# Sorting only the edge numbers and gathering the ends of the edges per tile, in a four-stage graph network

## The reference

```python
row, col = src, dst
edge_feature = silu(edge_rbf @ We1 + be1) @ We2 + be2     # 20625 x 128 -> 512
msg = edge_feature * x[col]                               # x is relu(layernorm(x)) here
agg = segment_sum(msg, row, num_segments=625)
return x + (silu(agg @ Wn1 + bn1) @ Wn2 + bn2)
```

## Time and profile before

| | |
|---|---|
| median of 3 runs | 1199.06 us |
| the profiled execution, its span | 1200.69 us, 1198.9 us |
| busy, share of the span | PE 97%, DVE 71%, ACT 57%, POOL 35% |
| chain that ended last | PE 88%, DVE 6%, ACT 3%, issue 1%, DMA 1% |
| granted TensorE clock, mean | 0.989 of full speed |
| HBM | 86.52 MB read, 8.85 MB written |

### The profile page before, as it was taken

One profiled execution on the slowest core, in us unless ns is written; L12 is line 12 of the kernel. 1 busy time (PEld: TensorE's weight loads), 2 busy tenths in 40 slices (PEclk: granted clock), 3 DMA queues, 4 the chain that ended last, 5 costly groups with the idle time before them and its releaser, 6 DMA issues.

```text
span 1198.9 us, 20918 instructions
## 1 busy us (share of the span) xinstructions
PE 1158.1 (97%) x6268; PEld 970.2 (81%) x6268; DVE 851.5 (71%) x1479; ACT 680.5 (57%) x1351; POOL 418.6 (35%) x546
## 2 busy tenths in 40 slices
PE   6989899999999999999999999998899999999997
PEld 3658788888888888888888888886789888798786
DVE  8767777777777777777777777777977234175664
ACT  3567567676676766767676676765734223142352
POOL 2001555565546555555555555551500000001000
PEclk9999999999999999999999999999899999999999
DMA  5544622222222222222222322221101202022101
GB/s 192 205 154 158 234 87 72 83 82 71 87 74 79 80 74 85 70 85 77 76 85 68 87 74 79 82 72 36 44 1 37 71 8 97 0 71 71 44 2 44
DMA packets 26966, 95.88 MB, mean 80 GB/s; under 512 B 6533, under 2 KB 6783, under 8 KB 22578
## 3 DMA queue, kind: packets, MB, share of 16 engines
q0 software_dynamic: 18592, 54.42, 15.2%
q1 hardware_dynamic: 8208, 40.84, 9.5%
q10 hardware_dynamic: 130, 0.13, 0.0%
HBM read 86.52 MB, written 8.85 MB: 80 GB/s over the span
## 4 chain that ended last, share of the span: by engine, by line
PE 88%; DVE 6%; ACT 3%; issue 1%; DMA 1%; DVEq 0%; SPq 0%; ACTq 0%
PE ps L1004 13%; PE ps L1006 12%; PE ps L1005 12%; PE ps L997 9%; PE ps L999 9%; PE ps L998 9%; PE ps L1012 3%; PE ps L1011 3%; PE ps L1111 3%; PE ps L1110 3%; PE ps L1050 3%; PE ps L1115 2%; PE ps L1038 1%; PE ps L1247 1%; PE ps L1065 1%
## 5 line engine op out<-in xcount | busy, mean ns | idle before, releaser
L1004 PE MATMUL ps<-we_hi,s_hi 128*128 128x512 f32 x664 | 268.7, 405 | 0.0
L1006 PE MATMUL ps<-we_hi,s_lo 128*128 128x512 f32 x664 | 260.2, 392 | 0.0
L1005 PE MATMUL ps<-we_lo,s_hi 128*128 128x512 f32 x664 | 260.1, 392 | 0.0
L578 POOL DMA_INDIRECT xg<-h_dram,node_picks x166 | 177.0, 1066 | 96.7 <-POOL node_picks L568 66.1
L720 ACT ACTIVATE m_hi<-msg 128x512 fp32r<-128x512 f32 x166 | 105.0, 632 | 156.9 <-DVE msg L1667 92.9
L572 POOL DMA_INDIRECT rbf<-in_edge,edge_picks x166 | 171.5, 1033 | 50.5 <-issue 33.5
L1672 DVE TENSOR_TENSOR m_lo<-msg,m_hi 128x512 fp32r<-128x512 f32 x166 | 114.9, 692 | 59.3 <-ACT m_hi L720 58.6
L1660 DVE TENSOR_TENSOR s_lo<-s,s_hi 128x1024 fp32r<-128x1024 f32 x83 | 101.8, 1226 | 75.5 <-ACT s_hi L714 50.3
L1006 PEld LDWEIGHTS ps<-we_hi,s_lo 128*128 128x128 f32 x664 | 124.9, 188 | 28.6
L1005 PEld LDWEIGHTS ps<-we_lo,s_hi 128*128 128x128 f32 x664 | 125.7, 189 | 21.1
L1004 PEld LDWEIGHTS ps<-we_hi,s_hi 128*128 128x128 f32 x664 | 125.3, 189 | 21.4
(11 more groups left out here) (301 smaller groups left out, 2556.4 us busy)
## 6 DMA issues: line engine op xcount, KB each, us to landing
stage<-in_fold_a SPq DMA_DIRECT2D x6, 1024.0 KB, 5.1
stage<-in_fold_b SPq DMA_DIRECT2D x6, 1024.0 KB, 8.6
fold_dram<-folded SPq DMA_DIRECT2D x6, 1024.0 KB
wstage<-fold_dram SPq DMA_DIRECT2D x6, 1024.0 KB, 4.9
w_raw<-in_nodew SPq DMA_DIRECT2D x3, 1024.0 KB, 7.2
wstage<-in_selfw SPq DMA_DIRECT2D x3, 1024.0 KB, 5.0
rbf<-in_edge,edge_picks POOLq DMA_INDIRECT x166
xg<-h_dram,node_picks POOLq DMA_INDIRECT x166
```

What stands on the lines that cost most here:

```text
L578: pool.indirect_dma_start(xg[t.slot][:, j], None, h_dram, bass.IndirectOffsetOnAxis(ap=node_picks[t.slot][:, j:j + 1], axis=0)).then_inc(x ...
L1004: pe.matmul(outp, lh, rh, start=False, stop=False, skip_group_check=True)
L1005: pe.matmul(outp, lh, rl, start=False, stop=False, skip_group_check=True)
L1006: return pe.matmul(outp, ll, rh, start=False, stop=False, skip_group_check=True)
```

## The change

- **Sorting.** Only the edge numbers are still moved by matmuls. `ended` and its multiplications on VectorE and matmuls on TensorE are gone. GpSimd writes both ends of all edges side by side (`ends_i`), and SyncE saves them as a table of 8 bytes per edge in DRAM (`ends_dram`), with a row ahead of the first for slots without an edge.
- **Gathers.** `slot_picks` has the edge number and the number plus one side by side. `gather_edges` issues two gathers of rows of the table (`ends`) ahead of the two of `rbf`; `pick_nodes` takes the destinations from `ends`.
- **Columns.** `srccol`, `dstcol`, `dstval` are made per step, two steps ahead (`column_firsts`, `column_seconds`), four VectorE operations on 128x2. The counts are packed as lower and upper half of the nodes instead of even and odd, so the flush reads its 16-bit halves with a stride.
- **Folds.** The three unsplit folds have buffers of their own (`plain`), and the factors of folds 0 to 4 are loaded at once. The last quarter of the factors of each split fold is split ahead of the marks and one-hots of that unit, not behind them.
- **Clearing.** `acc_agg` and half of `acc_adj` are cleared by GpSimd at the start, the rest later by VectorE.

```diff
@@ sync
             load_factors(0)
             load_factors(1)
             sp.dma_start(x_res[:], a["x"].rearrange("(c p) f -> p c f", p=NC)).then_inc(x_in, 16)
-            sp.wait_ge(fold_mm, K)
-            load_factors(2)
+            for m in range(2, FOLDS - 1):
+                load_factors(m)
+            sp.wait_ge(ends_joined, 4)
+            sp.dma_start(ends_dram[1:E + 1].rearrange("(p t) v -> p t v", p=EP), ends_i[:]).then_inc(ends_saved, 16)
+            sp.dma_start(ends_dram[0:1], no_ends[:]).then_inc(ends_saved, 16)
             save_product(0)
@@ gpsimd
+            pool.memset(acc_agg[:], 0.0).then_inc(acc_zeroed, 1)
+            pool.memset(acc_adj[:, 0:late_zero], 0.0).then_inc(acc_zeroed, 1)
...
             def pick_edges(t):
                 t.wait(pool, rT_mm, 1, -1)
-                pool.tensor_copy(edge_picks[t.slot][:], slot_edge[:, bass.ds(t.count(2), 2)]).then_inc(picked, 1)
+                t.wait(pool, cols_made, 4, -4)
+                pool.tensor_copy(edge_picks[t.slot][:].rearrange("p j v -> p (j v)"),
+                                 slot_picks[:].rearrange("p t v -> p (t v)")[:, bass.ds(t.count(4), 4)]).then_inc(picked, 1)
             def pick_nodes(t):
                 t.wait(pool, msg_ready, 2, -2)
-                pool.tensor_copy(node_picks[t.slot][:], slot_dst[:, bass.ds(t.count(2), 2)]).then_inc(picked, 1)
+                pool.wait_ge(ends_in[t.slot], t.rounds(32))
+                pool.sem_inc(ends_landed, 1)
+                pool.tensor_copy(node_picks[t.slot][:], ends[t.slot][:, :, 1]).then_inc(picked, 1)
             def gather_edges(t):
                 for j in range(2):
                     pool.indirect_dma_start(
+                        ends[t.slot][:, j], None, ends_dram,
+                        bass.IndirectOffsetOnAxis(ap=edge_picks[t.slot][:, j, 1:2], axis=0)).then_inc(ends_in[t.slot], 16)
+                for j in range(2):
+                    pool.indirect_dma_start(
                         rbf[t.slot][:, j], None, a["edge"],
@@ vector, hots(i)
-                for v in range(2):
-                    mm = dve.tensor_tensor(ended[r][:, v], hot_lo[r][:],
-                                           pairs[:, v, :, None].to_broadcast([EP, GROUP // 2, P, 2]), op=ALU.mult)
-                mm.then_inc(ends_made, 1)
@@ vector and scalar, the woven units
+                if u == K - 1 and WHOLE <= m + 1 < FOLDS:
+                    factor_low(m + 1, u)
                 if n + 1 < len(units):
                     for i in AFTER[units[n + 1][0]][units[n + 1][1]]:
                         hots(i)
...
-                if WHOLE <= m + 1 < FOLDS:
+                if u < K - 1 and WHOLE <= m + 1 < FOLDS:
                     factor_low(m + 1, u)
@@ vector, the edge step
+            def column_firsts(t):
+                s = t.slot
+                dve.wait_ge(ends_in[s], t.rounds(32))
+                t.wait(dve, hots_ready, 3, -3)
+                dve.tensor_tensor(srccol[s][:], ends[s][:, :, 0], tile_base[:, bass.ds(t.count(2), 2)],
+                                  op=ALU.subtract).then_inc(cols_made, 1)
+                dve.tensor_scalar(upper[s][:], ends[s][:, :, 1], float(ND), None, ALU.is_ge).then_inc(cols_made, 1)
...
                     rows_lo(t.at(2))
+                    column_firsts(t.at(2))
                 message(t, 0)
+                if ahead:
+                    column_seconds(t.at(2))
```

More of the change, by code:

```diff
@@ L264, in build @@
         iota_d = main("iota_d", [P, ND + 1], F16)
-        dstval = main("dstval", [P, TILES], F32)
-        odd_i = main("odd_i", [P, TILES], I32)
-        half_i = main("half_i", [P, TILES], I32)
         loop = Region(main.at)
-        edge_picks = [loop(f"edge_picks{i}", [P, 2], I32) for i in range(2)]
+        edge_picks = [loop(f"edge_picks{i}", [P, 2, 2], I32) for i in range(2)]
+        ends = [loop(f"ends{i}", [P, 2, 2], I32) for i in range(2)]
+        srccol = [loop(f"srccol{i}", [P, 2], F32) for i in range(2)]
+        upper = [loop(f"upper{i}", [P, 2], F32) for i in range(2)]
+        dstcol = [loop(f"dstcol{i}", [P, 2], F32) for i in range(2)]
+        dstval = [loop(f"dstval{i}", [P, 2], F32) for i in range(2)]
         node_picks = [loop(f"node_picks{i}", [P, 2], I32) for i in range(2)]
@@ L414, in build @@
         weights_hi, weights_lo = sem("weights_hi"), sem("weights_lo")
-        stage_in = [sem(f"stage_in{i}") for i in range(2)]
+        stage_in = [sem(f"stage_in{m}") for m in range(FOLDS)]
         split_hi, split_lo = sem("split_hi"), sem("split_lo")
@@ L468, in load_factors @@
             def load_factors(m):
+                factors = plain[m] if m < WHOLE else stage[m % 2]
                 for part, w in enumerate((a["fold_a"], a["fold_b"])):
-                    sp.dma_start(stage[m % 2][:, part].rearrange("p k f -> p (k f)"), w[m]).then_inc(stage_in[m % 2], 16)
+                    sp.dma_start(factors[:, part].rearrange("p k f -> p (k f)"), w[m]).then_inc(stage_in[m], 16)
             def save_product(m):
@@ L485, in _ @@
             sp.dma_start(row_a[:], a["be2"].to_broadcast([P, F])).then_inc(small_in, 16)
[L486 to L496, removed]
+            save_product(1)
+            sp.wait_ge(split_lo, K)
+            load_factors(FOLDS - 1)
+            sp.wait_ge(ln_act, 1 + C)
+            sp.dma_start(h_dram.rearrange("(c p) f -> p c f", p=NC), h32[:]).then_inc(h_saved, 16)
+            for m in range(2, FOLDS):
                 save_product(m)
@@ L1565, in hots @@
                                       op=ALU.is_equal).then_inc(made, 1)
-                pairs = ends16[:, :, i * GROUP:i * GROUP + GROUP].rearrange("p v (j u) -> p v j u", u=2)
-                dve.wait_ge(hots_lo_made, i + 1)
-                for v in range(2):
-                    mm = dve.tensor_tensor(ended[r][:, v], hot_lo[r][:],
-                                           pairs[:, v, :, None].to_broadcast([EP, GROUP // 2, P, 2]), op=ALU.mult)
-                mm.then_inc(ends_made, 1)
             def factor_low(m, k):
@@ L1703, in flush_agg, with dst_order, adj_rows @@
                 return b
+            def dst_order(pairs):
+                return pairs[:].bitcast(U16)[:, 0:NP].rearrange("p (n two) -> p two n", two=2)
+            def adj_rows(b):
+                return acc_adj[:, bass.ds(b * NP, NP)].rearrange("p (two n) -> p two n", two=2)
             def flush_adj(t, b):
@@ L1757, in edge_step @@
                     silu_lo(t.at(1))
-                if t.reg is not None or t.c + 2 < STEPS:
+                ahead = t.reg is not None or t.c + 2 < STEPS
+                if ahead:
                     rows_lo(t.at(2))
+                    column_firsts(t.at(2))
                 message(t, 0)
+                if ahead:
+                    column_seconds(t.at(2))
                 if full:
```

120 lines of the change are left out of this document (60 added, 60 removed).

## The result

The changed kernel takes 1254.24 us, the median of four runs (1247.66 to 1260.94), against 1199.27 of the kernel before on the same chip: 1.0463 times as long, 95% interval 1.0423 to 1.0503. Forecast were 1262, with a range of 1208 to 1298. The profiled execution is the one of 1249.35 us (span 1247.6).

A forecast was written before the change was run, and what follows sets the result against it. TensorE paced the loop before; GpSimd would after, at 9.33 us a step. Start, 80 steps, landing and tail gave +52.4, stalls +11: 1264.1 for the profiled execution, so 1262 us as median; range 1208 to 1298.

The forecast's parts named there:

- The table of edge numbers: Ahead of the loop: the table of edge numbers is complete at 93.2 us, 22.1 us before the earlier 115.34.
- The pace of the split folds: Ahead of the loop: about 5.2 us a unit instead of 6.08, as VectorE's two multiplications per group go.
- GpSimd's new work ahead of 19.46: Start of GpSimd's queue: new memsets and joining copies lie where it idled, in a wait of 13.70 us.
- An 8-byte gather costs as much as the others: Loop, GpSimd: each gather of 8 B a row takes 1.30 us, two 2.60 us a step; bounds 1.25 and 1.40.
- Rival 2: Loop, the two ends gathers: 8 B gathers are cheap, TensorE stays the pace, 1176 us; chance 0.14.
- The increment, 0.50: Loop, GpSimd: the new semaphore increment adds 0.50 us a step; bounds 0 and 0.50.
- rival 1: Loop, GpSimd: the increment is free and a gather costs the least, step 8.73 us, 1214 us in all; chance 0.14.
- The base of 6.23 and nothing for neighbours: Loop, GpSimd: its work before the change is 6.23 us a step, with 6.65 as upper bound.
- VectorE's additions, nothing: Loop, VectorE: four column operations, at most 1.0 us, and the strided flush fit into the new step, so count nothing.
- The GpSimd stalls, 4 x 2.7 = +11: Loop, GpSimd: a stall losing 2.7 us every 108 gathers, hidden before, comes four times exposed: +11 us.
- Start and tail: Around the 80 steps: first gathers done at 116.0 us; afterwards a landing of 2 us and a tail of 22.7.
- The clock (rival 3): Loop, TensorE: short idle gaps could halve its clock, step 9.8 us, 1300 us; chance 0.09, shared with dearer gathers and base.

The follow-up runs named there:

- before_plus2: Kernel before with two more 8-byte gathers per loop step, results unused, without the column operations or joined ends: 1286.79 us, ratio 1.0737.
- more_incs: Changed kernel with four more semaphore increments on GpSimd in each step, ahead of node_picks: 1256.39 us.
- late_memset: Changed kernel with GpSimd's two clearings of the sums moved behind the copies that join the ends: 1256.74 us in its one execution.
- slo_psum: Changed kernel with one operand of VectorE's s_lo read from a PSUM bank of zeros, all steps but the last three; output wrong: 1382.94 us.
- one_ends: Changed kernel with one gather of ends per step instead of two; output not the reference's: 1198.96 us.
- silu_psum: Changed kernel, complete, with silu written in place in PSUM and s_hi and s_lo reading it there: 1216.58 us, ratio 1.0112 to the kernel before.
- both_psum: Changed kernel, complete, with silu and also the messages written in place in PSUM, seeding of a bank waiting for m_lo: 1317.03 us.
- before_plus1: Kernel before with one more 8-byte gather per loop step, its result unused: 1206.63 us, ratio 1.0067.

## Why the prediction held, point by point

- **The table of edge numbers: 93.2 forecast, 96.5 found.** The pace of the split folds was right, 5.27 from one fold_lo to the next for 5.2, the answer to the earlier trace rows:

```profile
81.75 1.23 DVE L1580 TENSOR_TENSOR fold_lo<-stage,fold_hi 128x1024 fp32r<-128x1024 f32 x1 [1.94 <-ACT fold_hi L701]
87.02 1.22 DVE L1580 TENSOR_TENSOR fold_lo<-stage,fold_hi 128x1024 fp32r<-128x1024 f32 x1 [1.93 <-ACT fold_hi L701]
```

  What failed is the sentence that GpSimd's new work ahead of 19.46 lies where it idled. It did idle, but the clearings pushed its iotas beside VectorE's reach operations, and these took 3.95 us instead of 0.91:

```profile
4.92 3.95 DVE L1513 TENSOR_SCALAR reach<-src_f 125x165 f32<-125x165 f32 x4
96.23 0.24 DVE L1623 TENSOR_SCALAR slot_picks<-number 128x166 int32<-128x166 f32 x1
```

```profile
5.16 1.52 POOL L549 IOTA iota_lo<- 125x256 f16 x1
6.65 1.91 POOL L551 IOTA iota_hi<- 125x332 f16 x1
```

  Moving the clearings gave 1.9 of the 3.3 us back; the other 1.4 I can't place.
- **An 8-byte gather costs as much as the others: right.** 1.25 from start to start (I took 1.30). Rival 2, cheap gathers, is excluded by any step of the trace, and by before_plus2.
- **The increment, 0.50: wrong.** It costs nothing, as rival 1 said.
- **The base of 6.23 and nothing for neighbours: too low.** I had a step of before in which GpSimd never waited (6.65 in all) and took it only as an upper bound. Collisions cost up to 1.1 us in a step, of which 6.23 + 2.60 holds half: it is 8.83 against the collision-free 8.32. The missing half is what I gave the increment. So the step came out at 9.33 for 9.25 measured by two errors that cancel. That is luck: with the increment at nothing and the rest as it stands, a step would be 8.83 and the forecast 1222, 32 us below the measured time. What I saw on the copy alone, 0.87 us beside VectorE's flush, falls on the gathers too: the missing half.
- **VectorE's additions, nothing: right.** The four column operations take 0.15 to 0.17 us each and overlap, and the flush with its stride takes 0.80, as before.
- **The GpSimd stalls, 4 x 2.7 = +11: wrong.** Of the 2.7 us at 359.99, 1.0 were a collision: the gather of 1.98 ends at 361.97, 0.82 behind an s_lo that ran from 359.92 to 361.15, and the one at 811.68, after 1.89 us of idle, takes 0.95. And "every 108 gathers" doesn't carry over. In the changed kernel the loop has one, whose step takes 10.99 instead of 9.4:

```profile
590.42 1.25 POOL L598 DMA_INDIRECT xg<-h_dram,node_picks  x1 [1.41 <-issue]
```

- **Start and tail: right within 3 us.** gather(2) is done at 119.0 for 116.0, which is the late table. From there 80 steps end at 858.96, 9.25 each. The last transposes and the last scatter, the answer to the earlier trace rows:

```profile
861.68 0.33 PE L1082 MATMUL ps<-ident,rbf 128*128 128x128 f32 x1 [0.52 <-DMA rbf<-in_edge,edge_picks]
...
884.10 0.63 PE L1119 MATMUL ps<-m_lo,oh_src 128*125 128x512 f32 x1
```

  The landing took 2.7 (I had 2), the tail 23.1 (22.7). The edge phase ends at 884.7; the sum had 887.1 and 11 for stalls, 898.1. So 13.4 of the 14.7 us between 1264.1 and this execution's 1249.35 are there: 11 for the stalls and 6.4 for the steps too much, 3 for the start and 1 for landing and tail too little.
- **Rival 1 (8.73 a step)** is nearly what the loop does from 157 to 287 us, 8.64 a step, because the increment costs nothing and the gathers are lengthened by 0.25 us a step only. It doesn't last. How long it does differs from one execution to another: 15 steps in the execution of 1249.35, none with more_incs (a span of 1259.3), four with late_memset (1256.74). At 0.75 us a step, 15 steps are 11 us, about the spread of the changed kernel's runs; that this is its cause is argued, not shown.
- **The clock (rival 3)** stayed at 1.00 from 140 to 870 us, through 70 waits of TensorE for rbf with a mean of 0.8 us and a longest of 2.0. Of the two rules of the Trainium skill that I named, from "TensorE: Matmul & The Clock Gate", the second, frequent short waits throttling, did not come true here. The first, a long wait, has a case in slo_psum, where the clock fell to 0.50, the 1.2 GHz level, after 4.5 us of idle.

## What to carry to other kernels

Count a queue's instructions, not its bytes: an indirect gather costs GpSimd 1.25 us whether its rows have 8 bytes or 2048, so a table of 8-byte rows, bought to save some 11 us of work ahead of a loop, cost 80 x 0.9 = 72 us in it. When an engine that used to wait becomes the pace, take its step from what it does when it never waits, neighbours included, for its collisions were hidden in its waits. And split a change before judging it: the fold handling alone gave 1192.38.

## What the runs showed of the hardware

- **A gather that starts beside a VectorE operation with two SBUF inputs waits for its end** and finishes 0.80 to 0.86 us later (231 of 234 in the changed kernel, and pairs in before_plus2, one_ends, silu_psum and both_psum); one that has started 0.29 us ahead is not held (193.05). The Trainium skill, "SBUF — State Buffer", section "Who interferes with whom", says that such an operation contends with GpSimd's reads and that one with at most one SBUF input, outside VectorE's modes with two ports, does not; the traces agree, 1.53 against 0.97. The same section gives, as inferred, that a tensor_tensor does not stall the making of descriptors. For indirect gathers the 1.53 says otherwise, and the measurement decides. Their list of rows lies in SBUF; that it is the reading of this list that waits is my explanation, and no run isolates it.
- **It goes the other way too:** four VectorE operations on 125x165 with one input took 3.95 us beside two iotas of GpSimd, 1.04 without.
- **ScalarE and VectorE can start microseconds behind the recorded end of the matmuls that release them**, 6.6 us in the silu of slo_psum at 399.56, of which it had idled 3.4. It happens in five of the other kernels too (before_plus1, before_plus2, one_ends and both with the messages in PSUM), and in the loops of the rest not at all. VectorE's reading of PSUM alone doesn't make it (silu_psum has that and not this). The cause stays open.
